# Half items between two pairs of scores, and absolute sums on ScalarE, in a decoder layer's attention part

## The chip, the cores and the metric

The kernel runs on one core of a Trainium2 chip. The metric is the time of one launch on the device in microseconds, the median of several runs.

## The reference

`x` is 4 x 512 tokens of 512 features. The layer is `x = x + attention(layernorm(x))`, then `x = x + ffn(layernorm(x))`.

Each projection of the attention (q, k, v, o) uses the signs of its weight: `s = max(mean(|W|, axis=1), 1e-8)`, `y = nan_to_num((x @ sign(W / s).T) * s * scale)`, with infinities replaced by one million. There are 32 query heads and 8 key heads of 16 features; four query heads share a key head, and the softmax runs over 512 keys.

The feed-forward part takes three weights of 1792 x 512 (w2 transposed), each as `mean_w + mean(|w - mean_w|) * sign(w - mean_w)`, and computes `(silu(h @ W1.T) * (h @ W3.T)) @ W2.T`. So each weight needs one absolute mean over all of its differences, and the sign of each.

## The kernel before

The program is written per engine, with semaphores by hand. There are three parts: a start (weights' scales and signs, first batch's normalization and projections), the attention in 128 slices, and the feed-forward part.

**Slices.** A group `g` is one batch and one key head (32 groups); a slice `(g, kt)` is a quarter of its 512 keys. `at = 4 * (g % 8) + kt` is the slice's number within its batch, 0 to 31. TensorE's slice (`pe_slice`) holds: four shifted scores (`shifted_scores`, one of four query heads each, 50 rows deep, in one half of the array's rows, heads in `J_ORDER = (0, 2, 1, 3)`, so that neighbours lie in different halves); two plain pairs (`scores(n)`, `scores(n + 1)`, 48 rows deep), of which VectorE takes the row maxima (`maxima`) 14 pairs ahead; and the weighting of values by the slice before's probabilities (`weigh_values`, 32 columns each, four beside each other). ScalarE exponentiates each shifted score (L832). Maxima of a whole group are transposed (`transpose_maxima`, at kt == 1), split by VectorE (`split_shift`) and sent as two rows into the group's query slot by an 8 KB DMA (`load_shift`, L437), which the first shifted score of the next group waits for.

**Banks.** Shifted scores, transposed maxima and work beside share three PSUM banks in a ring, in the order of `ring_users`; a user waits until the one three places before has been read.

**Work beside.** While batch b is attended, batch b + 1 is prepared: four transposes of its tokens (at 0 to 3), six items (one projection tile of 128 features each, at 5, 8, 11, 14, 17, 20: `project_item`, eight products of 512 columns), and the values' transpose (at 24). It stands after the weighting and before the fourth shifted score. ScalarE scales an item (`scale_item`, L769), GpSimd guards it one slice later, VectorE selects (a predicated copy, L963) and GpSimd splits it three slices later, and SyncE stores it (`store_item`: three DMAs of 256 KB). In the last batch the output projection of batch 0 (`project`, at 16, 20, 24, 28) takes that place; VectorE scales, guards and adds it.

**Weights of the feed-forward part.** For each of 14 tiles `e`, SyncE loads three pieces of `w` and three of `mean_w` (`load_difference`, six DMAs of 256 KB), GpSimd subtracts all three pieces at once (L672, 1536 elements a partition), ScalarE takes Sign into `sgn` (L841) and Abs in place (L843), and GpSimd adds the magnitudes into `dacc` (L678). `weight_totals` reduces `dacc` in slice 119.

**SyncE.** It issues nearly all DMAs from one queue, group by group (`sp_group`): the next group's shift, the q and k loads of group g + 3, the store of weighted values (256 KB), item stores, tokens, differences, and at g == 3 and 5 the output factors (`load_factors`: single elements; `spread_factors`: 512 KB). The differences of tiles 0 and 1 are issued before group 0, later ones in even groups. In the last batch, at its slice 0, come the softmax sums, the tokens and weighted values of batch 0 (`load_sums`, `load_batch`), at its slice 4 the reciprocals, which go out to memory and come back as a broadcast (`load_reciprocals`).

**Start.** Scales and signs of q, then k and v; then tokens' transposes, six items, the values, and then the signs of the output weight; all before the first score. Transposed signs pass through four banks.

## Time and profile before

| | |
|---|---|
| median of 3 runs | 1053.17 us |
| lowest and highest | 1047.9, 1053.53 us |
| profiled execution | 1054.04 us |
| its span | 1052.0 us |
| granted TensorE clock, mean | 0.955 of full speed |
| busy: TensorE, VectorE, ScalarE, GpSimd | 968.0, 736.5, 538.8, 293.1 us |
| first exponential | 68.76 us into the span |

A row of a timeline or of the chain begins with the time since the span's start and a duration. A group's row ends with its busy time and the mean duration in ns, then the idle time before its instructions and what ended it. The clock is the share of full speed granted to TensorE: 1.00 is 2.4 GHz, 0.50 is 1.2 GHz, and a value between is a mean over time at both.

### The profile page before, as it was taken

Reading aid. Unit: us, or ns where it says so; the run is one execution under the profiler, and the core shown is the slowest. Engines: PE = TensorE matmul, PEld = TensorE weight load, DVE = VectorE, ACT = ScalarE, POOL = GpSimd, SP = SyncE. Lnnn points to the kernel's source line nnn. Section 1 sums busy time; section 2 is a strip of 40 time slices with the busy share of each in tenths; the row PEclk is TensorE's granted clock in tenths of the full one; section 3 lists DMA queues with packets and bytes.
Section 4 is the critical chain, followed back from the end, with each engine's and each line's share of the span. In section 5 each row is a group of like instructions: output and inputs, shape, how many; then the busy total and the mean of one; then the engine's idle time right before and its main releaser. Section 6 shows DMA issues by size and latency. Waiting matters only on the chain.

```text
span 1052.0 us, 14162 instructions
## 1 busy us (share of the span) xinstructions
PE 968.0 (92%) x4770; PEld 617.9 (59%) x4770; DVE 736.5 (70%) x978; ACT 538.8 (51%) x999; POOL 293.1 (28%) x247
## 2 busy tenths in 40 slices
PE   3588989999999989898889999999999999999997
PEld 2433433344344433333357888888888888888886
DVE  6585867888888787789695558855687557864443
ACT  3426768877897889574684331332223232232221
POOL 3134767566766642210000110101111110011110
PEclk9858998999999999688999999999999999999999
DMA  4535577455754575511494000240003300130001
GB/s 149 149 127 171 158 150 227 127 146 174 224 153 115 170 224 161 179 45 32 151 303 151 12 1 1 80 148 17 0 0 120 124 0 0 45 116 1 0 0 40
DMA packets 81361, 110.24 MB, mean 105 GB/s; under 512 B 10144, under 2 KB 33696, under 8 KB 81312
## 3 DMA queue, kind: packets, MB, share of 16 engines
q1 hardware_dynamic: 79152, 108.04, 33.8%
q10 hardware_dynamic: 2160, 1.58, 0.5%
q8 instruction: 27, 0.44, 0.2%
q14 instruction: 22, 0.18, 0.0%
HBM read 76.29 MB, written 32.78 MB: 104 GB/s over the span
## 4 chain that ended last, share of the span: by engine, by line
PE 70%; DVE 14%; DMA 5%; issue 3%; ACT 3%; SPq 3%; POOL 2%; DVEq 0%; ACTq 0%; POOLq 0%
PE psum L1389 15%; PE psum L1390 15%; PE psum L1391 14%; DVE nmx L994 8%; PE psum L1308 7%; PE psum L1298 7%; PE psum L1282 3%; DMA q_slot<-shift 3%; DVE g_alt L963 2%; PE psum L1319 2%; PE psum L1320 2%; PE psum L1225 1%; PE psum L1226 1%; ACT probs L832 1%; SPq L454 1%
## 5 line engine op out<-in xcount | busy, mean ns | idle before, releaser
L994 DVE TENSOR_REDUCE nmx<-psum 128x2 f32<-128x1024 f32 x256 | 300.9, 1218 | 74.6 <-PE psum L1282 74.3
L832 ACT ACTIVATE probs<-psum 128x512 f32<-128x512 f32 x512 | 276.1, 604 | 77.1 <-PE psum L1298 74.9
L1298 PE MATMUL psum<-q_slot,k_slot 50*128 50x512 f32 x512 | 172.0, 492 | 16.9 <-DMA q_slot<-shift 13.0
L1389 PE MATMUL psum<-fxh,wh 128*128 128x512 f32 x448 | 175.2, 391 | 2.2 <-DVE wl L1152 2.2
L1390 PE MATMUL psum<-fxl,wh 128*128 128x512 f32 x448 | 174.9, 390 | 0.0
L1391 PE MATMUL psum<-fxh,wl 128*128 128x512 f32 x448 | 174.7, 390 | 0.0
L719 POOL CAST dh<-w2T 128x512 fp32r<-128x512 f32 (+1 forms) x56 | 50.7, 906 | 430.1 <-PE psum L1391 393.5
L1298 PEld LDWEIGHTS psum<-q_slot,k_slot 50*128 50x128 f32 x512 | 77.5, 193 | 132.1 <-ACT probs L832 85.6
L1308 PE MATMUL psum<-probs,v_slot 128*32 128x512 f32 x1024 | 146.4, 646 | 0.7 <-ACT probs L832 0.7
L1282 PE MATMUL psum<-k_slot,q_slot 48*128 48x512 f32 x512 | 115.3, 465 | 26.7 <-DVE nmx L994 24.8
L1159 DVE TENSOR_TENSOR gate<-gate,psum 128x512 f32<-128x512 f32 x56 | 38.4, 686 | 133.6 <-PE psum L1391 131.3
L887 ACT ACTIVATE hh<-gate 128x512 fp32r<-128x512 f32 x56 | 35.4, 632 | 161.9 <-DVE gate L1159 161.9
L884 ACT ACTIVATE gate<-psum 128x512 f32<-128x512 f32 x56 | 33.5, 598 | 164.3 <-PE psum L1391 164.3
L1389 PEld LDWEIGHTS psum<-fxh,wh 128*128 128x128 f32 x448 | 84.5, 189 | 20.8 <-issue 2.9
L1390 PEld LDWEIGHTS psum<-fxl,wh 128*128 128x128 f32 x448 | 84.5, 189 | 17.6
L1391 PEld LDWEIGHTS psum<-fxh,wl 128*128 128x128 f32 x448 | 84.4, 188 | 17.7
L1282 PEld LDWEIGHTS psum<-k_slot,q_slot 48*128 48x128 f32 x512 | 57.1, 202 | 59.9 <-DVE nmx L994 53.8
L1389 PE MATMUL psum<-dh,hh 128*128 128x512 f32 x224 | 88.2, 394 | 0.1
L1390 PE MATMUL psum<-dl,hh 128*128 128x512 f32 x224 | 88.2, 394 | 0.0
L1391 PE MATMUL psum<-dh,hl 128*128 128x512 f32 x224 | 87.1, 389 | 0.0
L678 POOL TENSOR_TENSOR dacc<-dacc,stage 128x1536 f32<-128x1536 f32 x14 | 48.6, 3473 | 74.0 <-ACT stage L843 74.0
L1161 DVE TENSOR_TENSOR hl<-gate,hh 128x512 fp32r<-128x512 f32 x56 | 38.8, 692 | 39.8 <-ACT hh L887 39.8
(109 smaller groups left out, 1272.7 us busy)
## 6 DMA issues: line engine op xcount, KB each, us to landing
stage<-in_L_ffn_mean_w_dram SPq DMA_DIRECT2D x84, 256.0 KB, 4.6
q_slot<-q_stack SPq DMA_DIRECT2D x64, 192.0 KB, 3.5
stage<-in_L_ffn_w_dram SPq DMA_DIRECT2D x42, 256.0 KB, 4.8
q_stack<-q_hi SPq DMA_DIRECT2D x32, 256.0 KB
weighted_values<-u_sb SPq DMA_DIRECT2D x32, 256.0 KB, 3.8
k_slot<-k_stack SPq DMA_DIRECT2D x64, 96.0 KB, 3.6
xn<-_attn_hidden_states_dram SPq DMA_DIRECT2D x4, 1024.0 KB, 6.8
q_stack<-q_lo SPq DMA_DIRECT2D x16, 256.0 KB
```

The lines of the kernel that those rows point to most:

```text
L678: nc.gpsimd.tensor_tensor(dacc[:], dacc[:], mn[e % 2][:], ALU.add).then_inc(facc_ok, 1)
L719: nc.gpsimd.tensor_copy(dh[parity][:], w2T[:, bass.ds(src, 1), :].rearrange("p o c -> p (o c)")).then_inc(dh_ok, 1)
L832: nc.scalar.activation(probs[kt][:, j, :], BANK[ring_bank(("score", g, kt, j))], ACT.Exp, scale=HEAD_DIM ** -0.5).then_inc(exp_ok, 1)
L994: v.tensor_reduce(column, pair, AX.X, ALU.max, negate=True).then_inc(s_max, 1)
L1159: v.tensor_tensor(gate[:], gate[:], BANK[UP], ALU.mult).then_inc(h_ok, 1)
L1161: v.tensor_tensor(hl[p][:], gate[:], hh[p][:].bitcast(FP32), ALU.subtract).then_inc(hl_ok, 1)
L1282: last = mm(BANK[2 * jj + h], q_slot[s][rows, jj, q * P:(q + 1) * P], k_slot[s][rows, :], start=True, stop=True)
L1298: mm(BANK[ring_bank(("score", g, kt, j))], k_slot[s][rows, kt * P:(kt + 1) * P], q_slot[s][rows, jj, :], start=True, stop=True).then_inc(t ...
L1308: last = mm(psum[32 * j:32 * j + 32, 6, :], v_slot[g % V_SLOTS][:, kt, :], probs[kt][:, j, :], start=(kt == 0), stop=(kt == TT - 1))
L1389: mm(o, lhs_hi, rhs_hi, start=first, stop=False)
L1390: mm(o, lhs_hi, rhs_lo, start=False, stop=False)
L1391: return mm(o, lhs_lo, rhs_hi, start=False, stop=final)
```

## The change

- Order of a slice: shifted scores 1 and 2, plain pair n, work beside, plain pair n + 1, shifted scores 3 and 4, weighting, transposed maxima. The ring of banks follows that order. ScalarE reads the work beside after its second exponential, and copies the weighted values (`copy_u`) after its fourth.
- Items of batches 1 to 3 are projected and scaled in halves of 256 columns, in two slices; guard and prediction lags grow by one slice.
- GpSimd subtracts a tile's three pieces in three slices, beginning at 5 (it was 1) in place of one instruction. Abs writes its sum through `accum_out` into a column of `dsum`; the additions, `dacc` and its clearing go, and `weight_totals` reduces 3 x 14 numbers.
- SyncE issues the differences of tiles 0 and 1 within groups 0 and 1, later ones in odd groups; sums are loaded at slice 20 of batch 2, the tokens, weighted values and reciprocals at its slice 28. The attended values and projections begin earlier (projections at 11, 16, 20, 26 of the last batch).
- Start: weights of k and v come first, q's signs are made between the first items, transposed signs pass through two banks, and the output weight's scales come after the last item.

```diff
-GUARD_LAG, PRED_LAG = 1, 3
-VT_AT = 24
-INVERT_AT, ATTENDED_AT, PROJECT_AT, PROJECT_EVERY = 4, 10, 16, 4
-DIFF_AT = tuple(range(1, 112, 8))
-SIGN_LAG, ABS_LAG, SUM_LAG = 2, 5, 8
+GUARD_LAG, PRED_LAG = 2, 4
+VT_AT = 26
+INVERT_AT, ATTENDED_AT = 27, 4
+PROJECT_AT = (11, 16, 20, 26)
+HSEQ = SEQ // 2
+DIFF_AT = tuple(range(5, 112, 8))
+SIGN_LAG, ABS_LAG, SUM_LAG = 2, 5, 6
...
-    WEIGHT_SETS = ((QT, 4), (KTILE, 2), (OT, 4))
+    WEIGHT_SETS = ((KTILE, 2), (QT, 4), (OT, 4))
+    SIGN_BANK = (6, 7)
...
-        if at in ITEM_AT:
-            return "item", b, ITEM_AT.index(at)
+        for i in range(len(ITEMS)):
+            if 0 <= at - ITEM_AT[i] < 2:
+                return "item", b, i, at - ITEM_AT[i]
...
-            ring_users += [("score", g, kt, j) for j in J_ORDER[:3]]
+            ring_users += [("score", g, kt, j) for j in J_ORDER[:2]]
+            if beside(g, kt):
+                ring_users.append(beside(g, kt))
+            ring_users += [("score", g, kt, j) for j in J_ORDER[2:]]
             if kt == 1 and g < LAST_G:
                 ring_users.append(("max", g + 1))
-            if beside(g, kt):
-                ring_users.append(beside(g, kt))
-            ring_users.append(("score", g, kt, J_ORDER[3]))
...
-        for e in range(2):
-            load_difference(e)
...
+            if g < 2:
+                load_difference(g)
             for e in range(2, IT):
-                if 4 * g - 2 < DIFF_AT[e - 2] + SUM_LAG + 1 <= 4 * g + 2:
+                if 4 * g - 2 < DIFF_AT[e - 2] + SUM_LAG + 3 <= 4 * g + 2:
                     load_difference(e)
...
-            if b == BATCH - 1 and at == 0:
+            if b == BATCH - 2 and at == SLICES - 12:
                 for p in range(2):
                     sp.wait_ge(u_out[p], 16 * KV_HEADS // 2)
                 load_sums(0)
+            if b == BATCH - 2 and at == SLICES - 4:
                 sp.wait_ge(v_ok, BATCH)
+                for i in range(2, 5):
+                    sp.wait_ge(part_out[(5 * (BATCH - 1) + i) % Q_RING], stored(BATCH - 1, i))
                 load_batch(0)
-            if b == BATCH - 1 and at == 4:
                 load_reciprocals(0)
...
-        def difference(e):
-
-            pool.wait_ge(fw_in[e % 2], 96 * (e // 2 + 1))
-            nc.gpsimd.tensor_tensor(wn[e % 2][:], wn[e % 2][:], mn[e % 2][:], ALU.subtract).then_inc(fd_ok, 1)
-
-        def add_magnitude(e):
-
-            pool.wait_ge(fabs_ok, 3 * (e + 1))
-            positive(pool, facc_ok, e)
-            nc.gpsimd.tensor_tensor(dacc[:], dacc[:], mn[e % 2][:], ALU.add).then_inc(facc_ok, 1)
+        def difference(e, k):
+
+            if k == 0:
+                pool.wait_ge(fw_in[e % 2], 96 * (e // 2 + 1))
+            nc.gpsimd.tensor_tensor(wn[e % 2][:, k, :], wn[e % 2][:, k, :], mn[e % 2][:, k, :], ALU.subtract).then_inc(fd_ok, 1)
...
-                if j == J_ORDER[3]:
-                    if kt == 0 and g > 0:
-                        copy_u(g - 1)
-                    if beside(g, kt):
-                        beside_out(beside(g, kt))
+                if j == J_ORDER[2] and beside(g, kt):
+                    beside_out(beside(g, kt))
...
-                    nc.scalar.activation(mn[e % 2][:, k - 3, :], wn[e % 2][:, k - 3, :], ACT.Abs).then_inc(fabs_ok, 1)
+                    nc.scalar.activation(mn[e % 2][:, k - 3, :], wn[e % 2][:, k - 3, :], ACT.Abs,
+                                         accum_out=dsum[:, k - 3, e:e + 1]).then_inc(facc_ok, 1)
...
             for kt in range(KT):
-                mm(BANK[bank], signs[:, kt, w], xh[:, kt, :], start=(kt == 0), stop=False)
-                last = mm(BANK[bank], signs[:, kt, w], xl[:, kt, :], start=False, stop=(kt == KT - 1))
-            last.then_inc(q_mm, 1)
+                mm(BANK[bank][:, c], signs[:, kt, w], xh[:, kt, c], start=(kt == 0), stop=False)
+                last = mm(BANK[bank][:, c], signs[:, kt, w], xl[:, kt, c], start=False, stop=(kt == KT - 1))
+            last.then_inc(q0_mm if half == 0 else q_mm, 1)
...
             shifted_scores(g, kt, J_ORDER[0])
+            shifted_scores(g, kt, J_ORDER[1])
             if n < S_USES:
                 scores(n)
+            if beside(g, kt):
+                beside_in(beside(g, kt))
+            if n < S_USES:
                 scores(n + 1)
-            shifted_scores(g, kt, J_ORDER[1])
             shifted_scores(g, kt, J_ORDER[2])
+            shifted_scores(g, kt, J_ORDER[3])
```

## Rows read from the trace of the kernel before

**Rows 1.** The page: the span, and two groups of its table of costliest instructions.
```profile
span 1052.0 us, 14162 instructions
...
L994 DVE TENSOR_REDUCE nmx<-psum 128x2 f32<-128x1024 f32 x256 | 300.9, 1218 | 74.6 <-PE psum L1282 74.3
...
L678 POOL TENSOR_TENSOR dacc<-dacc,stage 128x1536 f32<-128x1536 f32 x14 | 48.6, 3473 | 74.0 <-ACT stage L843 74.0
```

**Rows 2.** Windows, L832 alone: length, busy (x), clock, DMA share, GB/s.
```profile
68.76:94.50 25.74, 10.85 (x20) 0.70 0.65 207
94.50:192.58 98.08, 58.30 (x109) 0.94 0.63 167
192.58:208.75 16.17, 10.78 (x21) 1.00 0.50 153
208.75:269.77 61.02, 36.80 (x68) 1.00 0.55 165
269.77:297.60 27.83, 21.64 (x40) 1.00 0.70 210
297.60:402.84 105.24, 69.14 (x129) 1.00 0.56 164
419.60:441.10 21.50, 8.76 (x17) 0.62 0.60 187
441.10:501.11 60.01, 32.09 (x62) 0.85 0.19 49
```

**Rows 3.** Timeline of a plain slice: start, us, instruction [idle before].
```profile
189.97 2.20 ACT L832 ACTIVATE probs<-psum 128x512 f32<-128x512 f32 x4
...
190.03 1.06 PE L1308 MATMUL psum<-probs,v_slot 128*32 128x512 f32 x8
...
191.03 0.62 PE L1298 MATMUL psum<-q_slot,k_slot 50*128 50x512 f32 x2
...
192.21 0.18 PEld L1298 LDWEIGHTS psum<-q_slot,k_slot 50*128 50x128 f32 x1 [0.26 <-ACT probs L832]
...
192.64 0.64 PE L1308 MATMUL psum<-probs,v_slot 128*32 128x512 f32 x4
```

**Rows 4.** Timeline of the slice with item 1 of batch 2.
```profile
221.65 0.40 PE L1225 MATMUL psum<-xh,signs_qkv 128*128 128x512 f32 x1
...
221.88 0.39 PE L1226 MATMUL psum<-xl,signs_qkv 128*128 128x512 f32 x1
...
222.21 0.50 PE L1298 MATMUL psum<-q_slot,k_slot 50*128 50x512 f32 x2
...
222.31 0.69 ACT L769 ACTIVATE yq<-psum,wstat 128x512 f32<-128x512 f32 x1 [1.17 <-PE psum L1226]
```

**Rows 5.** One line's instructions, L963: ns min/median/max.
```profile
L963 DVE COPY_PREDICATED g_alt<-g_mask,yq x24: 720/746/3601, 30.6 to 377.1; 128x512 f32<-128x512 int32 x24
```

**Rows 6.** The chain of waits: start, us, what; three of its transfers.
```profile
82.36 6.39 DMA q_slot<-shift
...
144.30 6.10 DMA q_slot<-shift
...
423.70 7.78 DMA q_slot<-shift
```

**Rows 7.** Timeline of SyncE alone, its DMA issues in groups 3 and 10.
```profile
127.00 1.16 SPq L437 DMA_DIRECT2D q_slot<-shift  x2
...
225.59 1.06 SPq L437 DMA_DIRECT2D q_slot<-shift  x2
...
236.11 0.43 SPq L455 DMA_DIRECT2D stage<-in_L_ffn_mean_w_dram  x1
```

**Rows 8.** DMA issues, single ones at 228.55, 236.11, 426.70: KB, us to landing.
```profile
weighted_values<-u_sb SPq DMA_DIRECT2D x1, 256.0 KB, 4.2
...
stage<-in_L_ffn_mean_w_dram SPq DMA_DIRECT2D x1, 256.0 KB, 6.0
...
reciprocals<-sums SPq DMA_DIRECT2D x1, 64.0 KB, 6.7
```

More of the change, by code:

```diff
@@ L115, in decoder_layer @@
     fac_row = keep("fac_row", [P, 2, KT, P])
+    sums = keep("sums", [P, P])
     dtot = keep("dtot", [P, 3])
@@ L176, in decoder_layer @@
     o_alt = late("o_alt", [P, SEQ])
-    sums = late("sums", [P, P])
     st2 = late("st2", [P, TT, 6])
@@ L368, in ring_free @@
             eng.wait_ge(xe_ok, 4 * (which[0] - 1) + which[1] + 1)
+        elif kind == "item" and which[2] == 0:
+            eng.wait_ge(y0_ok, NI * (which[0] - 1) + which[1] + 1)
         elif kind == "item":
@@ L698, in pool_slice @@
             for e in range(IT):
[L699 to L702 removed]
+                if 0 <= 4 * g + kt - DIFF_AT[e] < 3:
+                    difference(e, 4 * g + kt - DIFF_AT[e])
         for g in range(GROUPS):
@@ L780, in values_out @@
                                  BANK[bank].rearrange("p (t h d) -> p h t d", t=TT, d=HEAD_DIM), ACT.Copy).then_inc(v_ok, 1)
+        act.wait_ge(wstat_ok, 1)
+        for m in (KTILE, VTILE):
+            sign_tile(m)
+        for m in (KTILE, VTILE):
+            signs_out(m)
         for kt in range(KT):
@@ L784, in _ @@
             nc.scalar.activation(xh[:, kt, :], BANK[kt], ACT.Copy).then_inc(xh_ok, 1)
-        for i in range(NI):
-            scale_item(0, i, 4 + i % 3)
-            if i > 0:
+        act.wait_ge(wstat_ok, 2)
+        for m in (QT, QT + 1):
+            sign_tile(m)
+        signs_out(QT)
+        act.wait_ge(oscale_ok, 1)
+        scale_item(0, 0, 4)
+        signs_out(QT + 1)
+        for m in (QT + 2, QT + 3):
+            sign_tile(m)
+        hi_item(0)
+        for m in (QT + 2, QT + 3):
+            signs_out(m)
+        for i in range(1, NI):
+            scale_item(0, i, 4 + i % 2)
+            if i > 1:
                 hi_item(i - 1)
-        values_out(0, 7)
+        values_out(0, VT_BANK)
         act.wait_ge(wstat_ok, 3)
@@ L805, in beside_out @@
             elif kind == "item":
-                scale_item(b, which[0], bank)
+                scale_item(b, which[0], bank, which[1])
             elif kind == "vT":
@@ L833, in act_slice @@
                                      scale=HEAD_DIM ** -0.5).then_inc(exp_ok, 1)
+            if kt == 0 and g > 0:
+                copy_u(g - 1)
             k = 4 * g + kt - SLICES * (BATCH - 1) - ATTENDED_AT - 1
@@ L948, in _ @@
         weight_scales(0)
-        weight_scales(1)
         dve.wait_ge(rstd_ok, 1)
@@ L952, in _ @@
             v.tensor_scalar(xn[:, t, :], xn[:, t, :], mv[:, t, 0:1], rstd[:, t:t + 1], ALU.subtract, ALU.mult).then_inc(xn_ok, 1)
-        weight_scales(2)
+        weight_scales(1)
         dve.wait_ge(scl_in, 64)
         output_scales(slice(0, OT))
-        output_scales(slice(OT, WTILES))
-        dve.wait_ge(wstat_ok, 5)
+        dve.wait_ge(oscale_ok, 1)
         def select_item(b, i):
@@ L985, in _ @@
             guard(i)
+        weight_scales(2)
+        output_scales(slice(OT, WTILES))
         def maxima(nn):
@@ L1104, in dve_slice @@
                 split_shift(g + 1)
+            if b == BATCH - 2 and at == INVERT_AT:
+                invert_sums(0)
             if b == BATCH - 1:
-                if at == INVERT_AT:
-                    invert_sums(0)
                 if ATTENDED_AT <= at < ATTENDED_AT + KT:
@@ L1235, in transpose_values_in, with first_item @@
             last.then_inc(vT_mm, 1)
-        for m in range(OT):
+        def first_item(i):
+            positive(pe, yq_ok, i - 1)
+            project_item(0, i, 4 + i % 2)
+        for m in (KTILE, VTILE):
             transpose_signs(m)
-        pe.wait_ge(signs_ok, OT)
         pe.wait_ge(xn_ok, TT)
@@ L1242, in _ @@
             transpose_tokens(0, kt, kt)
+        pe.wait_ge(signs_ok, 1)
         pe.wait_ge(xl_ok, KT)
-        for i in range(NI):
-            positive(pe, yq_ok, i - 2)
-            project_item(0, i, 4 + i % 3)
-        transpose_values_in(0, 7)
+        first_item(0)
+        for m in (QT, QT + 1):
+            transpose_signs(m)
+        pe.wait_ge(signs_ok, 3)
+        first_item(1)
+        for m in (QT + 2, QT + 3):
+            transpose_signs(m)
+        pe.wait_ge(signs_ok, OT)
+        for i in range(2, NI):
+            first_item(i)
+        transpose_values_in(0, VT_BANK)
         for m in range(OT, WTILES):
@@ L1268, in beside_in @@
                     pe.wait_ge(xl_ok, KT * (b + 1))
-                project_item(b, which[0], ring_bank(user))
+                project_item(b, which[0], ring_bank(user), which[1])
             else:
@@ L1352, in pe_slice @@
                 transpose_maxima(g + 1)
-            if beside(g, kt):
-                beside_in(beside(g, kt))
-            shifted_scores(g, kt, J_ORDER[3])
             if 4 * g + kt == MEANS_SLICE:
```

91 lines of the change are left out of this document (43 added, 48 removed).

## Prediction

> **What bounds the kernel now.** I read the page first, then the windows by stretch of attention slices, then the timelines of one plain and one item slice, and last the chain of waits with SyncE's own timeline. The profiled execution took 1054.04 us over a span of 1052.0 us [rows 1], 0.9 us above the median of the three runs, 1053.17. The change touches the start (68.8 us before the first exponential [rows 2]) and the attention part; what follows keeps its code, and I carry it over unchanged. The reader is to see in the windows [rows 2] that the slices are not alike: 208.75 to 269.77 holds seventeen slices of batch 1 with its six items in 61.0 us, while the ten that follow need 27.8, and batch 0 and batch 3 hold stretches at a granted clock of 0.70, 0.62 and 0.85.
>
> A plain slice is bound by a loop of latencies, not by an engine [rows 3]: a shifted score starts at 191.03, its exponential ends with the four at 192.17, the product that reuses its bank starts at 192.21, the weighting of values at 192.64, and the weighting holds TensorE 1.00 us (190.03 to 191.03) before the next shifted score. 1.18 + 0.43 + 1.00 = 2.61 us. ScalarE steps by (2.20 - 0.60) / 3 = 0.53 us, so five instructions nearly fill it; VectorE's two maxima take 2.36 of it (1.218 each with their overlap [rows 1]). An item slice adds eight products at 0.23 us (221.65 to 221.88) behind the weighting, and the evacuation of 0.69 us at 222.31 stands in front of the last exponential [rows 4]: 1.0 + 1.9 + 0.3 + 0.6 + 0.6 + 0.5 = 4.9 us.
>
> The second bound is the DMA queue. A group cannot start before its shift has landed, an 8 KB transfer queued behind whatever SyncE issued before. The chain of waits holds it at 82.36 for 6.39 us, at 144.30 for 6.10 and at 423.70 for 7.78 [rows 6]; where nothing is ahead it isn't in the chain at all.
>
> **The change part by part.** *Order of a slice.* The two shifted pairs now stand together, the plain pairs between them, beside work in the gap. The loop of a plain slice only changes its member: the first shifted score gates the fourth where the last gated the third. Same 1.18 + 0.43 + 1.00, so 2.61 us and no gain. In exchange, ScalarE has 0.18 us of slack there. copy_u moves behind the fourth exponential, where it must wait for the weighting of the same slice; with a Sign or Abs behind it the next exponential starts some 0.6 us late (weighting over at 2.61, copy_u and one more to 2.68 + 2 x 0.53 = 3.74, where the score is ready at 2.61 + 0.54 = 3.15). Beside work hides that; in about fifteen plain slices it doesn't, against 0.3 us that copy_u costs now. Net 15 x 0.3 = 4.5 us, already inside the figures below.
>
> *Half items.* 18 items become 36 halves. No row shows a 256-column product: the step lies between half of 0.23 and all of it, 0.12 to 0.23 us; a weight load takes 0.18 us [rows 3], which hides behind a product of 0.23 now [rows 4] and may not fully behind a shorter one, so I take 0.13, eight are 1.05 us. A half slice then goes: shifted pair and plain pair 0.57, half item 1.05 with 0.1 to change over on either side, plain pair 0.23, shifted pair to weighting 0.45, weighting 1.0: 3.55 us (3.4 to 4.35 by the bounds). The scale needs between half of 0.69 us and all of it, and ScalarE has room for both. Twelve halves and five plain slices: 12 x 3.55 + 5 x 2.62 = 55.7 us for what takes 61.0 now, -5.3 us in each of three batches (from -7 to +4).
>
> The extra change-over is where a rule speaks against the change. The rows show 0.32 us from the last item product to the shifted score (221.88 to 222.21), 0.1 more than its step, and 0.43 us from a shifted score to the weighting, 0.2 more than a product's step [rows 3, 4]. The Trainium skill (TensorEngine Tiling (Array Packing), section Tiling Modes) says that a change of tiling mode drains the engine; half-height pairs, full products and quarter-width weightings are three modes, and the new order changes mode four times in a slice with beside work where the old one did three times. By the row's lower price this is the 0.1 us that I counted, by the upper 0.2: 55 such slices, 5.5 or 11 us.
>
> *GpSimd in pieces.* A difference over 1536 elements takes as long as the addition of that size, 3.47 us [rows 1]; three pieces take about 1.16 each. VectorE's predicated copy took 3.60 us once for each batch where its median is 0.75 [rows 5]; it can now be held 1.2 us at most. This is -2.4 us three times, in item slices, counted in the 55.7. The first Sign of a weight tile waits about 0.5 us now for a difference that stood behind an addition; that ends, too. The fourteen additions of 3.47 us vanish from an engine that nobody waits for but through those two: nothing more. In their place 42 Abs carry an accumulator. No row has one; from nothing up to a further step of 0.53 us. I take 0.15, inside the 0.18 of slack: nothing. Without that cover, 42 x 0.35 = 15 us at the upper end.
>
> *First loads.* 12 issues of differences, 3 MB, stand in front of the shift of group 1, which was issued at 82.36 and took 6.39 us [rows 6]; they move behind it. Slices 0 to 4 of batch 0 take 25.7 us, those of batch 1 16.2 [rows 2]; the start keeps its slow clock for three slices. I take 18.7: -7.0 us (bounds -9.5 and 0).
>
> *Start-up.* Keys and values first brings the first item about 1 us forward, but the item whose store is waited for, the second, is behind four sign transposes and comes no earlier; weight_scales(2) now stands between the last item and the signs of the output weights, and those pass through two banks in place of four. Its reduction runs over 2048 elements, twice a maximum's 1.218 us [rows 1]; a part lies beside the last transposes. +2.0 us (-1 to +3).
>
> *Where transfers now meet.* This is the term against. From issue of the shift at 225.59, the 832 KB of group loads and values store land at 228.55 + 4.2 = X + 7.2, and an item store and six differences, 2304 KB, at 236.11 + 6.0 = X + 16.5 [rows 7, 8]: 4.0 us for 1000 KB. ITEM_AT + PRED_LAG + 3 puts the stores of items 0 and 1 both at slice 12, and differences move to odd groups, so to the same SyncE group: 768 KB more, X + 20.5 with the costlier writes. Slices 14 to 19 leave 4 x 3.55 + 2 x 2.62 - 0.75 = 18.7 us. A stall of 1.8 us in batches 1 and 2 at slice 20, and by the same count 1.2 us at slice 28 (store, differences). In batch 0 the factors (4-byte pieces) follow: the shift landed at 144.30 + 6.10 = 150.4, 23.4 us after the issue at 127.00 [rows 6, 7], of which 10.5 are the other transfers, 12.9 theirs. Then X + 33: a stall of 14 us at slice 20, 3.5 at slice 28 with the broadcast, and 3.5 for the slower clock behind them. Slices 5 to 31: 55.7 + 27.7 = 83.4 clean; batch 0 104.4 for 98.1 (+6.3), batch 1 86.4 for 88.8 and 15.4 for 16.2 (-3.2), batch 2 the like with the sums' load (-2.9).
>
> In batch 3 the tokens, the attended values and the reciprocals now go in one SyncE group, and SyncE waits for the reciprocals' landing (6.7 us now, with the tokens' queue mostly drained [rows 8]) before the shift of group 25: tokens and values behind differences, X + 22; broadcasts issued to X + 25; the shift lands near X + 29. Six slices leave 15.6. A stall of 13 us and 3 of slow clock, where 419.60 to 441.10 shows 11 us above four plain slices. The projections, spread wider, save about 3 of the 16 us that the stretch from 441.10 to 501.11 loses now over its fifteen-odd slices, and copy_u takes 1.5 back: +3.6 us (-8 to +10).
>
> Sum: +2.0 - 7.0 + 6.3 - 3.2 - 2.9 + 3.6 = -1.2 us. 1054.0 - 1.2 = 1052.8, or 1052 on the scale of the medians.
>
> **The rivals.** *Forecast, gains eaten by transfers*: 1052 us, its own range 1047 to 1058. Chance 0.38.
>
> *Faster, the queue drains in time.* If small pieces run beside large ones on other DMA engines, the 14 and 13 us stalls fall to today's 5 and 8: 1052 - 14 = 1038, 1036 to 1047 in parts. For it: the store of items overlaps the factors in part. Against it: the three late shifts of the chain [rows 6] stand exactly where bulk was issued ahead of them. It decides if the shift of group 5 lands under X + 25. Chance 0.30.
>
> *Slower, half products aren't half price.* At 0.23 us a product a half slice is 4.35 us: 36 x 0.8 = 29 us, less some 8 that would have been stall anyway: 1052 + 21 = 1073; at 0.18, 1062. It decides above 0.16 us. Against it: weight loads overlap full products in the rows. Chance 0.14.
>
> *Slower, change-overs drain.* By the drain's upper price, + 5.5 us, together with 0.2 more at every other beside slice, +5: 1062. The page above is the one that would have it so. Chance 0.10.
>
> *Slower, the accumulator shows.* Above 0.33 us an Abs breaks through the slack; at 0.53, 42 x 0.35 = +15: 1067. Chance 0.08.
>
> **How the numbers follow.** The time is the likeliest case's. 1040 to 1066 leaves out the deeper half of the second case and the upper part of the last three, some 2 in 10. A measurement of this kernel tells about 0.5%, 5.3 us. Faster by more: the second case and a little of the first, 0.34. Slower by more: the last three, with the first's tail falling away, 0.28. Within: 0.38.
>
> **What the profile after would show.** Slices without beside work at 2.6 us and half slices at 3.4 to 3.7; products of 256 columns stepping by 0.13; no predicated copy above 2 us; slice 4 of batch 0 some 3 to 5 us earlier; a wait for the shift at slice 20 of batch 0 above 10 us; SyncE silent for over 8 us in front of the reciprocals' broadcast, and TensorE without work near slice 4 of batch 3. The prediction is wrong if those two stalls are small, or if half products step by over 0.16 us.

## The result, and the profile after

The changed kernel takes 1069.81 us (median of four runs, 1063.06 to 1079.53) where the kernel before takes 1050.54 (1046.11 to 1053.53): a ratio of 1.0166, 95% interval 1.0093 to 1.0238. It is slower by 1.7%. One of the four runs, 1079.53 us, fell into a slower state that some executions show, and every ratio here is taken without such runs. The prediction said 1052 with a range to 1066 and no measurable change; it was wrong. The profiled execution took 1070.86 us with a span of 1069.0, 17.0 above the span of [rows 1].

The page, the span and the group that answers to [rows 1]: the subtraction of one piece takes 1.28 us, a little over a third of 3.47.

```profile
span 1069.0 us, 14537 instructions
...
L680 POOL TENSOR_TENSOR stage<-stage 128x512 f32<-128x512 f32 x42 | 53.4, 1281 | 21.1 <-DMA stage<-in_L_ffn_mean_w_dram 21.1
```

Windows of the line of the exponentials, as in [rows 2]: length, busy (x), clock, DMA share, GB/s.

```profile
65.27:83.74 18.47, 10.65 (x20) 0.76 0.63 189
83.74:188.22 104.48, 57.32 (x108) 0.87 0.61 159
...
204.81:266.77 61.96, 36.42 (x68) 0.97 0.54 163
266.77:298.76 31.99, 20.83 (x40) 0.95 0.63 174
298.76:409.77 111.01, 67.89 (x129) 0.95 0.55 156
418.41:442.39 23.98, 6.29 (x13) 0.64 0.36 118
```

Set against [rows 2]: slices 0 to 4 of batch 0 fell from 25.74 to 18.47 us; its others rose from 98.08 to 104.48. The seventeen slices of batch 1 with its items, which were to fall from 61.02 to 57.5, take 61.96, and the ten behind them 31.99 for 27.83. Batch 2 takes 111.01 for 105.24. Batches 1 and 2, which never left full clock, now have stretches below it. In the last window, slices 3 to 5 of batch 3 alone take 23.98 us.

By part, measured against forecast: start -3.5 (+2.0); slices 0 to 4 of batch 0 -7.3 (-7.0); its other slices +6.4 (+6.3); batch 1 +5.5 (-3.2); batch 2 +5.8 (-2.9); batch 3 +7.4 (+3.6); what follows +2.7 (0). Sum +17.0 (-1.2).

The chain of waits, its transfers within the attention part. [rows 6] has three of those before.

```profile
133.48 8.08 DMA q_slot<-shift
166.30 6.99 DMA q_slot<-shift
250.77 6.43 DMA q_slot<-shift
278.52 7.14 DMA q_slot<-shift
361.62 6.65 DMA q_slot<-shift
393.74 3.21 DMA q_slot<-shift
414.52 10.21 DMA reciprocals<-sums
427.97 6.27 DMA q_slot<-shift
```

The late shifts are those of groups 5, 7, 13, 15, 21, 23 and 25, each the first issue behind an odd SyncE group, where the change put the differences; the odd groups that have neither an item store nor the sums or the batch beside them (1, 7, 9, 15, 17, 25) make none late. SyncE's own timeline shows what stood before the one at 250.77:

```profile
234.57 1.05 SPq L445 DMA_DIRECT2D q_slot<-shift  x2
...
239.20 0.62 SPq L403 DMA_DIRECT2D k_stack<-q_hi  x1
...
242.71 1.26 SPq L404 DMA_DIRECT2D q_stack<-q_hi  x1
...
245.42 2.39 SPq L462 DMA_DIRECT2D stage<-in_L_ffn_w_dram  x2
...
250.15 1.16 SPq L445 DMA_DIRECT2D q_slot<-shift  x2
```

Two item stores and six differences follow the shift of group 12 at 234.57. Some of the issues themselves are slow, 1.26 us for a store's where 0.62 is usual, so the next shift, whose two parts VectorE ends at 248.15 and 248.46, is issued only from 250.15 on; its last part, issued at 250.77, lands 6.43 us later, 22.6 us after 234.57.

### The profile page after: what moved, and what is told of

It is laid out like the page before. It is cut to its first block, busy times and chain, and to the rows that moved or that the text cites. A ratio compares the mean times of both kernels' runs of the same rounds, so it can differ in the third digit from the quotient of the medians.

```text
span 1069.0 us, 14537 instructions
## 1 busy us (share of the span) xinstructions
PE 968.4 (91%) x4914; PEld 622.0 (58%) x4914; DVE 730.6 (68%) x978; ACT 549.1 (51%) x1059; POOL 248.0 (23%) x260
## 4 chain that ended last, share of the span: by engine, by line
PE 70%; DVE 10%; DMA 8%; SPq 7%; issue 3%; ACT 2%; POOL 0%; DVEq 0%; ACTq 0%
PE psum L1416 14%; PE psum L1417 14%; PE psum L1418 14%; PE psum L1334 7%; PE psum L1324 7%; DVE nmx L1008 5%; PE psum L1308 4%; DMA q_slot<-shift 4%; SPq L462 2%; PE psum L1239 2%; PE psum L1345 1%; PE psum L1346 1%; PE psum L1240 1%; DMA reciprocals<-sums 1%; DMA stage<-in_L_ffn_mean_w_dram 1%
## 5 line engine op out<-in xcount | busy, mean ns | idle before, releaser
L1008 DVE TENSOR_REDUCE nmx<-psum 128x2 f32<-128x1024 f32 x256 | 304.0, 1220 | 98.2 <-PE psum L1308 95.9
L843 ACT ACTIVATE probs<-psum 128x512 f32<-128x512 f32 x512 | 271.1, 600 | 111.7 <-PE psum L1324 111.1
L1324 PE MATMUL psum<-q_slot,k_slot 50*128 50x512 f32 x512 | 155.2, 493 | 45.5 <-DMA q_slot<-shift 35.2
L1324 PEld LDWEIGHTS psum<-q_slot,k_slot 50*128 50x128 f32 x512 | 68.5, 196 | 169.0 <-ACT probs L843 65.1
L1308 PEld LDWEIGHTS psum<-k_slot,q_slot 48*128 48x128 f32 x512 | 53.6, 205 | 43.3 <-DVE nmx L1008 29.8
L680 POOL TENSOR_TENSOR stage<-stage 128x512 f32<-128x512 f32 x42 | 53.4, 1281 | 21.1 <-DMA stage<-in_L_ffn_mean_w_dram 21.1
```

The lines of the kernel that those rows point to most:

```text
L680: nc.gpsimd.tensor_tensor(wn[e % 2][:, k, :], wn[e % 2][:, k, :], mn[e % 2][:, k, :], ALU.subtract).then_inc(fd_ok, 1)
L843: nc.scalar.activation(probs[kt][:, j, :], BANK[ring_bank(("score", g, kt, j))], ACT.Exp, scale=HEAD_DIM ** -0.5).then_inc(exp_ok, 1)
L1008: v.tensor_reduce(column, pair, AX.X, ALU.max, negate=True).then_inc(s_max, 1)
L1308: last = mm(BANK[2 * jj + h], q_slot[s][rows, jj, q * P:(q + 1) * P], k_slot[s][rows, :], start=True, stop=True)
L1324: mm(BANK[ring_bank(("score", g, kt, j))], k_slot[s][rows, kt * P:(kt + 1) * P], q_slot[s][rows, jj, :], start=True, stop=True).then_inc(t ...
```

## The experiments

All kernels are edits of the changed one except e8, which edits the kernel before, and e9 and e10, which edit e6. The ratio is always to the kernel before, timed on the same chip, where its median lay between 1047.4 and 1053.2 us; the changed kernel has 1.0166. "Slices 19 to 21" and the like are read from the windows between the first exponentials of those slices.

**e1, differences split over two groups.** Part 1 is the three pieces of w, part 2 the three of mean_w.

```diff
-                    load_difference(e)
+                    load_difference(e, 1)
+                if 4 * g - 2 < DIFF_AT[e - 2] + SUM_LAG + 7 <= 4 * g + 2:
+                    load_difference(e, 2)
```

> Edit to the changed kernel: of each tile from the third on, the three pieces of w are loaded in the odd group as now, the three of mean_w one group later, so that no group issues more than 768 KB of them. Theory (the queue: 1536 KB of differences behind item stores make the shift late in groups 13, 15, 21, 23): all waits for the shift in batches 1 and 2 but the one behind the sums vanish, 3.2 + 2.6 us in batch 1 and 4.0 + 1.5 in batch 2, with the 2.4 + 1.1 and 3.3 + 1.0 of slow clock behind them, about -18 us; batch 0 -3 (the shift is issued without waiting for the queue), batch 3 -3 (768 KB fewer ahead of the reciprocals): 1046 us. Rival (stores of half items alone, or the shorter slices, are what makes it late): the waits shrink by a third, 1064 us.

Measured: 1052.46 us, ratio 1.0005 (0.9965 to 1.0044); all that the change had lost is back. Windows of slices 19 to 21 and 27 to 31, batch 1, then batch 2, line of the exponentials:

```profile
248.70:263.39 14.69, 6.39 (x12) 0.77 0.59 178
278.00:291.93 13.93, 10.30 (x20) 1.00 0.76 201
...
355.65:365.70 10.05, 6.38 (x12) 1.00 0.78 244
380.44:395.63 15.19, 10.30 (x20) 1.00 0.84 225
```

The changed kernel has 14.77, 17.57, 16.56 and 16.34 us there. Three of the four fell; slices 19 to 21 of batch 1 did not: with two stores and only three differences the shift still lands 21.3 us after the one before it was issued (22.6 with six). In batch 2 the same transfers let it land after 19.4 us (23.2 with six), and its slices 19 to 21 are clean. In the profiled runs whose transfers there are the changed kernel's, these two figures lie between 20.9 and 23.2, so batch 1 alone shows little. The gain is 17 us of the 24 expected; why the load of batch 1 stayed late where that of batch 2 did not isn't shown.

**e12, item stores apart.** The other half of the same group, taken out alone.

```diff
+STORE_AT = (8, 12, 16, 20, 24)
...
-                    if at <= ITEM_AT[i] + PRED_LAG + 3 < at + 4:
+                    if at == STORE_AT[i]:
```

> The changed kernel with one edit: its item stores go one to each SyncE group (at 8, 12, 16, 20, 24 in place of two at 12 and then 16, 20, 24); differences, factors and reciprocals stay. Theory (from the issue of the shift of group 12 to the landing of the next it takes 22.6 us with two stores and six differences; one store fewer takes 3.5 to 4.2 off): the waits before slice 20 of batches 1 and 2, 3.2 and 4.0 us, go with the 2.4 and 3.3 of slow clock behind them, those before slice 28 stay; batch 0 loses 4 of its stall: -16 us, 1054. Rival (the queue is at its limit over a whole batch, so the wait is put off to slice 28): -5, 1065.

Measured: 1055.93 us, ratio 1.0043 (0.9999 to 1.0087). The same four windows:

```profile
252.67:262.72 10.05, 6.39 (x12) 1.00 0.48 139
277.12:294.69 17.57, 10.32 (x20) 0.81 0.52 148
...
358.44:368.50 10.06, 6.40 (x13) 1.00 0.48 143
382.90:397.67 14.77, 10.31 (x20) 1.00 0.65 169
```

Slices 19 to 21 are clean in both batches (the shifts land after 18.7 and 19.2 us), slices 27 to 31 of batch 1 not a bit shorter: the theory's pattern and its size (-14 of -16). The rival, that the wait is only put off, falls in batches 1 and 2; in batch 0 slices 19 to 21 gain 3.1 us, and slices 27 to 31 lose 1.3 of them. One store fewer in the group is enough in both batches, three differences fewer in batch 2 alone.

**e3, whole items in the new order.**

```diff
-        for i in range(len(ITEMS)):
-            if 0 <= at - ITEM_AT[i] < 2:
-                return "item", b, i, at - ITEM_AT[i]
+        if at in ITEM_AT:
+            return "item", b, ITEM_AT.index(at), None
```

> Edit to the changed kernel: items whole again (eight products of 512 columns in one slice, one scale instruction), everything else kept, the lags too. Theory (the half items bring the 2.4 us that slices 5 to 18 of batch 1 gained, 47.19 against 49.63, and the queue eats it): slices 5 to 18 go back to about 49.5, the waits for the shift of groups 13 and 21 shrink by as much, the total is within 3 us of the changed kernel's 1070. Rival 1 (it is the order that gains, the halving costs change-overs): slices 5 to 18 stay at 47 or fall, total 1066 or less. Rival 2 (halving gains and the queue does not care): total 1077.

Measured: 1068.69 us, ratio 1.0211 (1.0134 to 1.0287), not to be told from the changed kernel. Windows of slices 5 to 18, batches 1 and 2:

```profile
209.27:257.93 48.66, 29.60 (x56) 1.00 0.57 169
...
321.42:368.71 47.29, 29.49 (x56) 1.00 0.51 149
```

The changed kernel has 47.19 and 47.14, the kernel before 49.63 and 49.15. So my theory, that halving carries the 2.4 us, is false in batch 2, where whole items give 1.9 of the 2.0: rival 1 by the slices, though not by its total (1066 or less). In batch 1, where VectorE has the tokens' statistics beside, halving gives 1.5 of the 2.4.

**e10, whole items with a free queue.** e3's edit, as shown there, on e6 (below).

> The kernel with the spread queue and short factors in group 2, with whole items (eight products of 512 columns in one slice, one scale). Theory (the halving is worth 1.5 us in a batch where VectorE has the tokens' statistics beside, 0.2 where it has not, as slices 5 to 18 say: 48.66 and 47.30 us whole, 47.20 and 47.14 halved): +3 to +5 us over the 1028 of the same kernel with halves. Rival (the halves' gain was hidden by the late shifts and is larger with a free queue): 1036 or more. Rival 2 (none): 1028.

Measured: 1037.49 us, ratio 0.9881 (0.9794 to 0.9968), against 0.9790 of e6; the intervals overlap. The profiled execution took 1048.62 us, the longest of the four, so it is compared in stretches at full clock alone: slices 5 to 18 take 48.67 and 47.31 us in batches 1 and 2 (e6: 47.17 and 47.17), slices 19 to 21 10.82 and 10.83 (e6: 10.08 and 10.05), and batch 0, whose slices 5 to 18 e6 spoils with its factors, is like batch 1 against e9 (49.26 to 47.47, 10.82 to 10.04). Halving is worth 2.2 us in batch 1, 0.9 in batch 2, 2.6 in batch 0, some 5.7 in all. That is more than the theory's 3 to 5, and less than the 9 by which the medians differ; what the rest of those 9 is isn't shown.

**e8, the order alone on the kernel before.** TensorE's, ScalarE's and the ring's order only.

```diff
             shifted_scores(g, kt, J_ORDER[0])
+            shifted_scores(g, kt, J_ORDER[1])
             if n < S_USES:
                 scores(n)
+            if beside(g, kt):
+                beside_in(beside(g, kt))
+            if n < S_USES:
                 scores(n + 1)
-            shifted_scores(g, kt, J_ORDER[1])
             shifted_scores(g, kt, J_ORDER[2])
+            shifted_scores(g, kt, J_ORDER[3])
```

> Edit to the kernel before: only the order of a slice, its ring of banks and ScalarE's order are the changed kernel's; items whole, additions, lags, loads and start as before. Theory (the order gains in item slices, as the changed kernel with whole items shows in batch 2, 47.30 us for slices 5 to 18 against 49.14): slices 5 to 18 of batches 1 and 2 fall by 1.0 to 1.8 us each, the total by 3 to 5: 1048. Rival (what gains there are GpSimd's pieces and the missing additions, and the order costs copy_u): slices 5 to 18 within 0.5 us of before, total 1051 to 1056.

Measured: 1056.45 us, ratio 1.0056 (1.0013 to 1.0099), a little slower. Windows of slices 5 to 18 of batches 1 and 2, and of slices 16 to 30 of batch 3, where the kernel before has 57.63 us at a clock of 0.88:

```profile
208.22:257.04 48.82, 29.62 (x56) 1.00 0.51 148
...
313.90:362.15 48.25, 29.51 (x56) 1.00 0.45 128
...
458.71:522.98 64.27, 31.54 (x61) 0.84 0.21 65
```

The item slices gain 0.8 and 0.9 us a batch, a little under the theory; slices 16 to 30 of batch 3, with the projections at their old places, lose 6.6, while batch 3 as a whole is 3.6 longer. The changed kernel, with projections moved, has 55.71 us there. So the new order loses with the old places of the projections, which the prediction did not see; the new places with the old order were not run.

**e4, Abs without its accumulator.** The kernel leaves the absolute sums out: they are set to a constant once.

```diff
-                    nc.scalar.activation(mn[e % 2][:, k - 3, :], wn[e % 2][:, k - 3, :], ACT.Abs,
-                                         accum_out=dsum[:, k - 3, e:e + 1]).then_inc(facc_ok, 1)
+                    nc.scalar.activation(mn[e % 2][:, k - 3, :], wn[e % 2][:, k - 3, :], ACT.Abs).then_inc(facc_ok, 1)
```

> Edit to the changed kernel: Abs without its accumulator; the sums are left out (dsum is set to a constant once), the rest kept. Theory (the second instruction of 0.20 us that each of the 42 Abs brings lies in ScalarE's slack in plain slices, and shows only in the few slices with copy_u, a scale or a second Sign): slices of 4.07, 4.02 and 3.71 us shorten by 0.2 or less, total -1 to -3 us, 1068. Rival (it breaks through the slack): 42 x 0.23 = -10 us, 1060.

Measured: 1070.29 us, ratio 1.0191 (1.011 to 1.0272): no gain. The price itself is in the changed kernel's trace, one line's instructions, min/median/max in ns:

```profile
L856 ACT ACTIVATE stage<-stage x42: 621/634/669, 102.8 to 498.3; 128x512 f32<-128x512 f32 x42
L856 ACT ACTIVATION_READ_ACCUMULATOR stage<-stage x42: 192/202/241, 103.3 to 498.8; 128x1 f32 x42
```

Each Abs brings a second instruction of 0.20 us, within the bounds of nothing to 0.53 and close to the 0.15 that I took. Slices 5 to 18 become 0.11 to 0.19 us shorter a batch without it, 0.45 us over three: hidden. The Trainium skill (ScalarE activation tables: per-element evaluation and per-set limits, section What a function is on this engine) says that whichever table is read, the same operands, the accumulator output among them, cost the same; it says nothing on what the output itself adds, which is this row.

**e5, 1024 elements in place of 2560.**

```diff
-            sp.dma_start(fac_dram.rearrange("a w p -> p a w"), wstat[:, 3:5, :],
-                         allow_slow_non_contiguous=True).then_inc(fac_out, 16)
+            for a in range(2):
+                sp.dma_start(fac_dram[a, OT:].rearrange("w p -> p w"), wstat[:, 3 + a, OT:],
+                             allow_slow_non_contiguous=True).then_inc(fac_out, 16)
```

> Edit to the changed kernel: the factors' transfer takes only the output weight's columns, 1024 single elements in place of 2560, in two issues at the same place. Theory (the time of this transfer goes by its elements, 12.9 us by the trace of the kernel before, and stands in front of the shift of group 5): it falls to some 5.2 us, the stall of 8.6 us at slice 19 of batch 0 to about 1, with 2 to 3 us of slow clock behind it: 1060 us. Rival (the two item stores and six differences alone do it): the stall stays above 6 us, 1068.

Measured: 1071.49 us, ratio 1.0219 (1.0151 to 1.0288): no gain, and the theory that the time goes by the elements is gone. The shift of group 5 lands 28.2 us after the issue of the one before it, 27.8 with all elements. The edit also makes two transfers of one, so the number of elements is not all that differs. All engines' windows around it, of the changed kernel (DMA share and GB/s are the last two numbers):

```profile
134.00:136.00 2.00, 0.00 (x0) 0.00 (x0) 0.00 (x0) 0.00 (x0) 0.69 (x1) 0.91 0.69 28
136.00:140.00 4.00, 0.00 (x0) 0.00 (x0) 0.00 (x0) 0.00 (x0) 0.00 (x0) 0.50 0.39 3
```

For four microseconds with everything waiting, the queue moves 3 GB/s; in e5 it is 36 GB/s from 138 to 142. Part of the delay arises at the issue: behind the factors, the first part of the shift takes SyncE 3.77 us where 0.57 is usual, and in e5, whose factors are two issues, the second of these takes 2.72. The Trainium skill (DMA: Bandwidth & Descriptors, section Specifications) says that transfers below 512 B are done as read-modify-write; it would explain slow elements, but not that 1024 of them delay the shift as much as 2560. Why they do stays open.

**e11, the factors ahead of the first shift.**

```diff
+        load_factors()
         load_shift(0, 0)
...
-            if g == 3:
-                load_factors()
```

> The changed kernel with one edit: the factors (all 2560 elements) are issued ahead of the first shift in place of group 3. Theory (they stop the queue for about 6 us whatever their number, in front of the shift of group 5): the stall of 8.6 us at slice 19 of batch 0 falls to the 3 us of the same place in batch 1, the slices 19 to 21 from 22.9 to 15 us: 1062, less 0 to 3 if the first shift is late for it. Rival (the stores and differences alone are the cause): 22 us there, 1070.

Measured: 1066.86 us, ratio 1.0201 (1.0125 to 1.0277). The shift of group 5 now lands 23.3 us after its predecessor's issue, as in batch 1 (22.6): the factors cost 4.5 us there, not 12.9. Slices 19 to 21 take 19.40 us for 22.87. The first shift becomes late instead (it lands 4.35 us after its issue, 1.74 in the changed kernel), and the start takes 66.75 for 65.27. Theory right in kind, half in size.

**e2, the batch's transfers one group later.**

```diff
-INVERT_AT, ATTENDED_AT = 27, 4
-PROJECT_AT = (11, 16, 20, 26)
+INVERT_AT, ATTENDED_AT = 27, 8
+PROJECT_AT = (15, 19, 23, 27)
...
-            if b == BATCH - 2 and at == SLICES - 4:
+            if b == BATCH - 1 and at == 0:
                 sp.wait_ge(v_ok, BATCH)
```

> Edit to the changed kernel: tokens, attended values and reciprocals of batch 0 are issued one group later (slice 0 of batch 3 in place of slice 28 of batch 2), attended values at 8, projections at 15, 19, 23, 27. Theory (SyncE waits 10.2 us for the reciprocals in front of the shift of group 25): the 14.1 us stall at slice 3 of batch 3 vanishes with some 2 us of slow clock; what moves is in front of the shift of group 26, whose slices are longer: a stall of 0 to 4 us. 1056 us. Rival (the stall only moves by a group, as the kernel before has it in front of its slice 7): 1063 to 1068 us.

Measured: 1066.09 us, ratio 1.016 (1.0084 to 1.0236): the rival. Windows of slices 3 to 5 and 6 to 10 of batch 3 (changed kernel: 23.98 and 15.51), and the shift of group 26 in the chain:

```profile
423.16:431.90 8.74, 6.18 (x12) 1.00 0.90 268
431.90:459.62 27.72, 10.54 (x21) 0.66 0.56 167
...
439.23 6.69 DMA q_slot<-shift
```

**e7, the reciprocals' store first.**

```diff
                 load_shift(g + 1, (s + 1) % 4)
+            if b == BATCH - 2 and at == SLICES - 4:
+                store_reciprocals(0)
```

> Edit to the changed kernel: the reciprocals' store is issued first in SyncE's group 23, ahead of differences, tokens and values; their broadcast stays behind them. Theory (the stall of 14.1 us before slice 4 of batch 3 is in part SyncE's wait of 10.2 us and in part 3.5 MB in front of the shift): the shift is issued some 10 us earlier but lands only 5 us earlier, -5 us: 1065. Rival 1 (the bytes alone): within 1 us of 1070. Rival 2 (the wait alone): -13, 1057.

Measured: 1068.17 us, ratio 1.0164 (1.0093 to 1.0236). Slices 3 to 5 take 20.42 us for 23.98, slices 6 to 10 17.61 for 15.51. The wait for the reciprocals is out of the chain, and in its place the shift takes longer behind the bytes:

```profile
426.20 9.98 DMA q_slot<-shift
```

Theory on the stall (-3.6 of -5), nothing on the whole. e2 and e7 together say that neither the place nor SyncE's wait alone makes this stall: the bytes in front do it also without the wait (e7), and bytes and wait together do it one group later as well (e2).

**e6, the queue spread.** All compute of the changed kernel; e1, e12, short factors in group 2 and their broadcast in group 8, the reciprocals' store first in group 23, values, broadcast and tokens in groups 23, 24 and 25.

```diff
+            if b == BATCH - 2 and at == SLICES - 4:
+                store_reciprocals(0)
...
-                load_batch(0)
-                load_reciprocals(0)
+                load_values(0)
+            if b == BATCH - 1 and at == 0:
+                spread_reciprocals(0)
+            if b == BATCH - 1 and at == 4:
+                load_residual(0)
```

> Edit to the changed kernel, all of its compute kept: every SyncE group gets at most one item store (items stored in the groups at 8, 12, 16, 20, 24) and three pieces of a tile (w in odd groups, mean_w in even ones); short factors in group 2, their broadcast in group 8; the reciprocals are stored first in group 23, and values, broadcast and tokens of batch 0 go in groups 23, 24 and 25, attended values at 8, projections at 15, 19, 23, 27. Theory (everything that the change lost, it lost to shifts that land late): nearly no wait for a shift is left; batch 0 104, batches 1 and 2 102 each, batch 3 109, start and rest as they are: 1020 us. Rival (the waits move to other groups, since the queue is as full as before): 1045 us.

The lines shown are a part of the edit. Measured: 1028.12 us, ratio 0.979 (0.9721 to 0.9859). It beats both kernels, and misses the expected 1020 by 8 us. Windows: slices 5 to 18 of batch 0; 19 to 21 and 27 to 31 of batch 1; 3 to 5 of batch 3:

```profile
84.25:136.62 52.37, 29.94 (x56) 0.93 0.66 158
...
239.38:249.46 10.08, 6.40 (x13) 1.00 0.76 204
265.94:279.88 13.94, 10.30 (x20) 1.00 0.76 203
...
394.39:403.14 8.75, 6.22 (x13) 1.00 0.79 246
```

Not one shift is more than half a microsecond late. The batches take 110.0, 104.3, 104.0 and 107.8 us (kernel before: 123.8, 105.0, 105.2 and 116.2, the last without its last slice). So batches 1 and 2, where the kernel before hardly waits for a shift, are only about 1 us shorter each than in the kernel before; the gain over it lies in batches 0 and 3, where its own transfers held it up, and in the start. The kernel before with its queue spread was not run, so how much of the 2.1% needs the compute edits is open. The first window is most of what is left; single slices are long, too, among them 25 of batch 1 (4.96 us where batch 2 has 2.81) and 31 of batch 2 (4.44 for 2.61). In the first window, behind the factors in group 2 the shift of group 4 lands 0.5 us late, and the load of keys behind it holds the plain pairs, as the chain has it:

```profile
117.76 8.27 DMA k_slot<-k_stack
```

**e9, e6 with the factors at the start.**

```diff
+        load_factors()
         load_shift(0, 0)
...
-            if g == 2:
-                load_factors()
```

> The kernel with the spread queue (one item store and three pieces of a tile for each group, reciprocals first), in which the short factors are issued ahead of the first shift in place of group 2. Theory (after a run of single elements the queue moves hardly anything for some 6 us, so that the shift of group 4 took 6.4 us and the slices 5 to 18 of batch 0 took 52.37 us where batch 1 needs 47.17): slices 5 to 18 of batch 0 take 47.5, and the start is at most 1 us longer: 1023 us. Rival (the shift of group 4 is late for the item store in front of it): no gain, 1028; second rival (the first shift is late instead): start +4, 1027.

Measured: 1031.05 us, ratio 0.9821 (0.9743 to 0.99): the second rival. Slices 5 to 18 of batch 0 fall to 47.47 us, and the start grows from 65.67 to 68.30, since the first shift now takes 5.69 us.

Batches 1 to 3, which have the same code in both, take 3.6, 1.6 and 2.1 us longer in e9's profiled execution, at 1036.17 us the longest of its four. I take this for a spread between executions; no run settles it.

## Why the prediction was wrong, step by step

**What bounds the kernel** was read rightly: the loop of 2.61 us a plain slice is unchanged, and the queue is the second bound. That the gains of the slices would be eaten by transfers was the forecast; what failed is how much the queue takes.

**The size of the stalls in batches 1 and 2** is the step that failed first. The prediction counted 1.8 us at slice 20 and 1.2 at slice 28, from "X + 20.5" and 4 us for each 1000 KB. Here X is the issue of the shift before. The shift landed at X + 22.6 in batch 1 and X + 23.2 in batch 2, and 2 us more on 20.5 are enough to double a stall that is the difference to the 18.7 of the work. Slice 19 took 5.78 us and slice 27 5.24 where 2.61 is a plain slice, 3.2 and 2.6 us of stall in batch 1 (4.0 and 1.5 in batch 2). e12 takes a 768 KB store away and wins the whole wait in both batches; e1 takes 768 KB of loads away and wins 3.8 us of landing in batch 2 and 1.3 in batch 1. Whether a store costs more than its bytes is not settled by these.

**The slow clock behind a stall** is the term that was missing there. The prediction charged it in batches 0 and 3 only. Here are the stall and the slice behind it, slices 19 and 20 of batch 1, same line and columns as the windows above:

```profile
252.00:257.78 5.78, 2.06 (x4) 1.00 0.95 251
257.78:263.48 5.70, 2.17 (x4) 0.70 0.39 150
```

And slice 20 of batch 1 in e6, behind no stall:

```profile
241.98:246.16 4.18, 2.17 (x4) 1.00 0.74 206
```

TensorE did next to nothing in most of the first window; in the second its granted clock is 0.70, part at 2.4 and part at 1.2 GHz, and the slice takes 5.70 us where the same slice takes 4.18 at full clock. So a stall of 3.2 us costs 4.7, and one of 2.6 costs 3.6 (slice 28 takes 4.31 for 3.31). The expectations of e1 and e12 put the slow slices higher, since they were measured there against other slices. Over batches 1 and 2 the stalls measured 11.3 us and the slow slices 5.9, against 6.0 forecast: 11 of the 17.4 us by which the two batches were missed. Of the rest, 2.4 us lie in slices 0 to 4, which were to gain 0.8 a batch and lost 0.4, 3.1 in slices 5 to 21 without their stalls (next part), and some 1 in the ten behind them.

**Half items.** The half product's step was sized well, the gain of the item slices too high:

```profile
208.42 0.19 PEld L1240 LDWEIGHTS psum<-xl,signs_qkv 128*128 128x128 f32 x1
208.54 0.28 PE L1240 MATMUL psum<-xl,signs_qkv 128*128 128x256 f32 x1
...
208.66 0.28 PE L1239 MATMUL psum<-xh,signs_qkv 128*128 128x256 f32 x1
...
209.25 0.28 PE L1240 MATMUL psum<-xl,signs_qkv 128*128 128x256 f32 x1
...
209.46 0.50 PE L1308 MATMUL psum<-k_slot,q_slot 48*128 48x512 f32 x2
209.56 0.47 ACT L765 ACTIVATE yq<-psum,wstat 128x256 f32<-128x256 f32 x1 [0.38 <-PE psum L1240]
```

208.54 to 208.66 is 0.12 us for one, a shade under the 0.13 taken and half of 0.23; the load of 0.19 us hides. From the last of them to the plain pair it is 0.21 us, 0.1 over the step: the lower price of a change-over, as counted. A drain of the kind that the Trainium skill describes (TensorEngine Tiling (Array Packing), section Tiling Modes) costs no more than that at this change-over. The half slices take from 3.29 to 4.18 us at full clock, 3.62 in the mean, where 3.55 was forecast (from terms that add up to 3.50); the five slices between them take 13.9 us for 13.1. So without stalls slices 5 to 21 need 57.2 us (e6) and not 55.7: the term of -5.3 us a batch was -3.8. And the gain was put down to the wrong edit: e10 against e6 and e9 shows that halving brings 5.7 us in three batches. The order of the slice alone brings 0.8 and 0.9 us a batch (e8); the rest is left to GpSimd's pieces and missing additions, which no run took by themselves. The step that said "no gain" for the order looked at plain slices only.

**GpSimd in pieces**: the longest predicated copy takes 0.91 us, where [rows 5] has 3.60; as forecast (in e6 one takes 1.73).

**First loads**: right in kind and size (-7.3 for -7.0); the wait for the shift of group 1 is out of the chain.

**Batch 0 behind them**: +6.4 for +6.3, right by luck. The stall before slice 20 measured 8.6 us, not 14, and under the 10 that the prediction named as its sign: the factors cost 4.5 us in front of that shift and not 12.9 (e11). But the slow slices 20 and 21 add 4.2, where 3.5 was charged for all of the batch, and the stall before slice 28 with its slow slices brings 3.0 + 1.2 + 1.6. Together that is 18.6 us for 21, and the clean slices 5 to 31 take 85.9 for 83.4, which makes up for it.

**Batch 3**: the stall near its slice 4 was forecast at 13 us and measured 14.1 (slice 3, 16.70 us). SyncE was silent for 9.8 us before the broadcast, as the prediction said to look for. The shift landed 29.8 us after its predecessor's issue, forecast X + 29. That the whole is +7.4 and not +3.6 lies mostly in the projections: the stretch from slice 16 on gains 1.9 us where 3 were counted, while slice 11, which now holds the first projection, takes 5.40 us and slice 15, behind VectorE's addition of it, 6.24, where 3.64 and 3.89 were before.

**Start**: the step that failed is "comes no earlier". The chain of waits within the start, of the kernel before and then of the changed one, has these rows; the first scores begin at 52.44 and at 48.95:

```profile
36.77 7.36 DMA q_stack<-q_lo
```

```profile
32.86 6.45 DMA q_stack<-q_lo
...
41.39 2.18 DVE wstat L948
```

The second item's store is issued 3.9 us earlier and lands 4.8 earlier (39.3 for 44.1): its sign tiles are two of four, and the first item begins at 21.3 for 25.2. The reduction of 2.18 us that stands between the last item and the signs was forecast (2 x 1.218) and is in the chain; of the 4.8 us, 3.5 are left at the first scores.

**What follows** was carried over unchanged and took 2.7 us more. In the chain the last store of weighted values takes 4.09 us where it took 2.02; for the rest no experiment was made.

**Rivals.** "The queue drains in time" is refuted for the changed kernel, and its test was the right one: the shift of group 5 landed at X + 27.8, over the X + 25 named. The three slower rivals were all about engines (half products, change-overs, accumulator), and all three are refuted by rows. The time came out among theirs (1062 to 1073), for a reason that none of them named. What was missing was a rival in which the stalls of batches 1 and 2, with the slow slices behind them, cost nearly three times as much (17.2 us for 6.0).

## What to carry to other kernels

Before moving transfers in a hand-ordered queue, add up for each group what stands between one urgent small transfer and the next, and the time that the work leaves; an edit that makes the work shorter shrinks that room, and two bulk items that fall into one group can cost more than the edit brings (e12 and e1 win back 14 and 17 us here by moving 768 KB out of a group). Charge a long stall of TensorE twice: once for the wait and once for the slice behind it at a lower granted clock. When a change mixes compute and queue edits, time the compute edits with the queue spread: here the same compute goes from 1.7% slower to 2.1% faster. And spread the queue of the kernel before as well, the run that is missing here, or the compute edits get the credit for what the queue alone would give.

## What the runs showed of the hardware that was not expected

- 1024 single-element writes in two transfers and 2560 in one delayed the next shift about equally (it lands 28.2 and 27.8 us after the issue of the one before, 23.3 without them); for 4 us the core's queue moved 3 GB/s with all 2560, and 36 GB/s in e5. With 1024 of them in front, a shift landed 6.4 us after its issue in e6 and 5.7 at the start in e9, where 1.7 is usual.
- Some of SyncE's issues slow down while transfers are under way, from 0.62 to between 1.3 and 1.5 us for a 256 KB store in the changed kernel, so that the next shift is issued late as well as landing late. Other stores, at 253.69, were issued in 0.63 us although the DMA engines were busier (DMA share 0.95 in that slice, 0.50 from 241.14 to 245.3); what decides it isn't shown.
- An ACTIVATE with an accumulator output is two rows, 0.63 and 0.20 us.
- A stall of 3.2 us was followed by a slice at a granted clock of 0.70, which took 5.70 us where 4.18 is its time at full clock.
